# A graph and expert kernel: product of the router from raw rows, result biases kept in SBUF, last stage in groups of 3, 7 and 4 tiles

## The chip, the cores and the metric

The kernel runs on one core of a Trainium2 chip. The metric is the device time of one execution in microseconds (us), lower is better. Engines are written as in the profile: PE is TensorE, PEld its weight loads, DVE VectorE, ACT ScalarE, POOL GpSimd, SP SyncE, which here only starts transfers. A small q behind a name is that engine's instruction queue.

## The reference, cut to what matters

6250 nodes with 256 features and 200,000 edges. First comes a graph attention over the edges, then a mixture of 16 experts of which each node uses two.

```
x = x + gnn(layernorm(x), src, dst, edge_attr)       # edge stage, then one division per node and head
z = layernorm(x)
logits = z @ gate_w + gate_b                         # 6250 x 16
topk_vals, topk_idx = top_k(logits, 2);  topk_w = softmax(topk_vals)
h = relu(z @ w1[e] + b1[e])                          # 256 -> 512, for the two experts e of a node
expert_out = h @ w2[e] + b2[e]                       # 512 -> 256
y = z + sum over the two of topk_w * expert_out
x = x + layernorm(y) * gamma + beta
```

## The kernel before, in words

Nodes lie in 49 tiles of 128 rows; the last has 106 real rows. `token_rows` holds all of them in SBUF. All engines run queues of their own, in an order written by hand, and wait on counted semaphores. The stages follow each other:

*Edge stage.* Gathers rows for 200,000 edges and sums messages per node into `acc`. The diff doesn't touch it.

*Routing* (`stage_nodes`), seven groups i of seven tiles. ACT copies the sums to `staged` (L1027), four buffers; PE transposes them (L1076, `sums`); DVE divides (L1154) and adds the residual into `token_rows` (L1161), then takes statistics (L1228, L1234). ACT takes the square root (L1057), DVE the inverse, ACT writes the normalised rows `xn` (L1043), two buffers of seven tiles. PE transposes `xn` (L1108), ACT copies that (L1049), PE multiplies by the gate weights (L1093, `product`). DVE adds the gate bias (L1193) and finds the best two (`best_two`); PE counts how many rows go to each expert (`counts`), ACT copies the totals, DVE computes slots in HBM (`slots`), and POOL scatters the rows of the group to `dispatched` by 14 indirect transfers (L1011). In a step i, DVE does slots(i-1), attention and statistics(i+1), best_two(i), inverse(i+1); PE does counts(i-1), sums(i+1), router(i); ACT totals(i-1), stage(i+1), xn(i), the copies of i and deviation(i+1). `xn` of group i waits until the scatter of group i-2 has landed. SP loads b1, beta and the second weights of all experts (16 transfers of 512 KB, L962) once the last sums have been staged, because these lie in `shared`, in the place of `acc`. Then it stores 17 blocks of padding rows (L971).

*Experts* (`stage_experts`). 104 tiles of 128 dispatched rows, sorted by expert, in turns of four (R5). PE's step j: first layer of tile j+1 (L1512), transposition of the rows of j+2 (L1501), second layer of j (L1522). DVE's step j: rectified half of j+1, its flags and weights (L1548 to L1571), then for tile j the bias addition (L1577) and the weighting with the own row into `ys` (L1582). ACT does the other half, the own row (L1485) and copies. POOL scatters `ys` to `expert_rows` (L1375) and adds beta to `token_rows` (L1381) in 49 of the steps. SP's step j starts three transfers for tile j+3, in this order:

```
after(sp, s_h, j - R5 + 1);  first weights, 512 KB      # here j stands for the tile that is loaded
after(sp, s_t, ...); after(sp, s_bi, ...); after(sp, s_own, j - R5 + 1);  rows xs, 129.5 KB
after(sp, s_ys, j - R5 + 1);  result bias b2_t, broadcast to 128 partitions, 128 KB
```

Once in a turn SP reads eight numbers (experts and rows of four tiles) into registers (`load`, L1366); DVE, ACT and PE read one for every tile.

*Last stage.* In seven groups of seven tiles: SP loads the two expert rows of every node, `y0` and `y1`, two buffers deep. POOL adds four tiles (L1700); for the other three ACT copies `y1` to PSUM (L1679) and DVE adds (L1721). Statistics on DVE (L1728, L1734), square root (L1683), inverse, normalising on ACT (L1687) into four PSUM banks, gamma on DVE (L1744), the residual with beta on POOL (L1708), then SP stores.

## Time and profile before

| What | us |
|---|---|
| median of 3 runs | 2765.64 |
| lowest and highest | 2764.18, 2768.57 |
| the profiled execution | 2765.15 |
| span of its instructions | 2763.0 |
| PE busy | 943.2 |
| DVE busy | 1178.0 |
| ACT busy | 757.5 |
| POOL busy | 1794.8 |

The profiled execution is one more run; its span goes from the first to the last instruction. Busy times are summed over the whole span, most of which is the edge stage, so they say little on the stages that the diff touches. Those are read from stretches of the trace.

### The profile page before, as it was taken

Reading aid. Unit: us, or ns where it says so; the run is one execution under the profiler, and the core shown is the slowest. Engines: PE = TensorE matmul, PEld = TensorE weight load, DVE = VectorE, ACT = ScalarE, POOL = GpSimd, SP = SyncE. Lnnn points to the kernel's source line nnn. Section 1 sums busy time; section 2 is a strip of 40 time slices with the busy share of each in tenths; the row PEclk is TensorE's granted clock in tenths of the full one; section 3 lists DMA queues with packets and bytes.
Section 4 is the critical chain, followed back from the end, with each engine's and each line's share of the span. In section 5 each row is a group of like instructions: output and inputs, shape, how many; then the busy total and the mean of one; then the engine's idle time right before and its main releaser. Section 6 shows DMA issues by size and latency. Waiting matters only on the chain.

```text
span 2763.0 us, 40902 instructions
## 1 busy us (share of the span) xinstructions
PE 943.2 (34%) x6693; PEld 862.8 (31%) x6694; DVE 1178.0 (43%) x4381; ACT 757.5 (27%) x2809; POOL 1794.8 (65%) x1923
## 2 busy tenths in 40 slices
PE   6311222222222211122222222211126559899860
PEld 6211111111111111111111111111126458888850
DVE  5533333333333333333333333333347656666646
ACT  3222222222222222222222222222234323333334
POOL 3677777777777777777777777777735643333326
PEclk8555555555555555555555555555555579999985
DMA  5222222222222222222222222222212667676656
GB/s 170 60 57 56 56 57 56 56 57 56 56 57 56 56 57 56 56 56 56 56 57 56 57 56 56 57 56 56 57 28 78 216 204 222 213 220 217 218 183 225
DMA packets 191305, 260.90 MB, mean 94 GB/s; under 512 B 64374, under 2 KB 133047, under 8 KB 191140
## 3 DMA queue, kind: packets, MB, share of 16 engines
q0 software_dynamic: 59872, 135.05, 19.8%
q1 hardware_dynamic: 124980, 122.05, 14.4%
q10 hardware_dynamic: 6416, 3.41, 0.4%
q8 instruction: 11, 0.18, 0.0%
q14 instruction: 26, 0.21, 0.0%
HBM read 222.54 MB, written 38.69 MB: 95 GB/s over the span
## 4 chain that ended last, share of the span: by engine, by line
POOL 53%; issue 21%; PE 8%; DMA 6%; DVE 5%; SPq 4%; ACT 2%; POOLq 1%; DVEq 0%; ACTq 0%
POOL rows L206 52%; DMA xs<-dispatched 4%; SPq L1366 3%; PE p_y L1522 2%; PE p_h L1512 2%; PE p_l L1093 1%; POOL dispatched L1011 1%; ACT xn L1043 1%; PE p_tab L407 1%; DMA shared<-expert_rows 1%; DMA dispatched<-xn,slot_i 1%; ACT staged L1027 1%; PE p_t L1108 1%; PE p_x L1501 0%; SPq L1416 0%
## 5 line engine op out<-in xcount | busy, mean ns | idle before, releaser
L206 POOL DMA_INDIRECT rows<-node_table,index x1568 | 1480.2, 944 | 533.0 <-issue 477.3
L688 PE MATMUL p_win<-hot_ex,msg 128*65 128x64 f32 x3136 | 393.8, 319 | 1559.2 <-DVE hot_ex L801 1170.5
L688 PEld LDWEIGHTS p_win<-hot_ex,msg 128*65 128x65 f32 x3136 | 359.6, 229 | 1593.3 <-issue 1187.6
L723 ACT ACTIVATE p_part<-rows,attr_all 128x64 f32<-128x64 f32 x1568 | 388.4, 299 | 1495.2 <-DMA rows<-node_table,index 1495.2
L770 DVE TENSOR_TENSOR part<-rows,p_attr 128x544 f32<-128x544 f32 x196 | 141.3, 721 | 870.4 <-DMA rows<-node_table,index 868.8
L763 DVE TENSOR_TENSOR shared<-shared,p_win 65x64 f32 x784 | 171.0, 218 | 394.4 <-issue 312.7
L1375 POOL DMA_INDIRECT expert_rows<-ys,back x104 | 102.0, 981 | 308.6 <-DVE ys L1582 240.9
L1512 PEld LDWEIGHTS p_h<-xt,shared 128*128 128x128 f32 x1664 | 203.4, 193 | 5.4
L1512 PE MATMUL p_h<-xt,shared 128*128 128x128 f32 x1664 | 203.9, 276 | 0.0
L1522 PE MATMUL p_y<-shared,hid_t 128*128 x832 | 197.6, 381 | 0.0
L1522 PEld LDWEIGHTS p_y<-shared,hid_t 128*128 128x128 f32 x832 | 149.9, 190 | 16.3
L1011 POOL DMA_INDIRECT dispatched<-xn,slot_i x98 | 99.4, 1014 | 77.2 <-issue 41.5
L797 DVE TENSOR_TENSOR msg<-part,p_part 128x512 f32<-128x512 f32 x196 | 132.6, 677 | 0.0
L801 DVE TENSOR_TENSOR hot_ex<-hot,p_ex 128x512 f32<-128x512 f32 x196 | 132.6, 677 | 0.0
L1467 ACT ACTIVATE hid_t<-p_h,shared 128x128 f32<-128x128 f32 x208 | 64.9, 363 | 174.2 <-PE p_h L1512 174.1
L1548 DVE TENSOR_SCALAR hid_t<-p_h,shared 128x128 f32<-128x128 f32 x208 | 63.4, 346 | 96.4 <-PE p_h L1512 94.6
L1577 DVE TENSOR_TENSOR p_y<-p_y,b_t 128x256 f32<-128x256 f32 x104 | 45.0, 432 | 54.6 <-PE p_y L1522 54.0
L1501 PE MATMUL p_x<-ident,xs 128*128 128x128 f32 x208 | 42.0, 284 | 70.8 <-DMA xs<-dispatched 70.8
L1485 ACT ACTIVATE own<-xs,is_first 128x256 f32<-128x256 f32 x104 | 52.6, 506 | 27.2 <-DVE is_first L1559 25.9
L1582 DVE SCALAR_TENSOR_TENSOR ys<-p_y,weight,own 128x256 f32<-128x256 f32 x104 | 50.3, 484 | 20.8 <-DVE p_y L1577 20.6
L1454 ACT ACTIVATE xt<-p_x 128x256 f32<-128x256 f32 x104 | 39.9, 383 | 62.8 <-PE p_x L1501 62.8
L779 DVE TENSOR_TENSOR hot<-dst_rel,p_dve 128x128 f32<-128x128 f32 x196 | 54.8, 280 | 0.0
(221 smaller groups left out, 1254.0 us busy)
## 6 DMA issues: line engine op xcount, KB each, us to landing
shared<-in_w SPq DMA_DIRECT2D x120, 512.0 KB, 6.3
rows<-node_table,index POOLq DMA_INDIRECT x1568
xs<-dispatched SPq DMA_DIRECT2D x104, 129.5 KB
b_t<-in_b SPq DMA_DIRECT2D x104, 128.0 KB, 4.1
shared<-expert_rows SPq DMA_DIRECT2D x14, 768.0 KB, 6.3
out<-shared SPq DMA_DIRECT2D x6, 896.0 KB, 4.1
token_rows<-in_x SPq DMA_DIRECT2D x5, 896.0 KB, 7.2
index<-in_src SPq DMA_DIRECT2D x196, 4.0 KB, 1.6
```

What stands on the lines that cost most here:

```text
L206: pool.indirect_dma_start(out=rows[:, s, k, :], out_offset=None, in_=table, in_offset=bass.IndirectOffsetOnAxis(ap=index[:, s, k:k + 1], a ...
L688: last = pe.matmul(psum[0:MSG, u * HEADS * W:(u + 1) * HEADS * W], msg[:, v, k, :], weighted[:, k, :, :].rearrange("p h w -> p (h w)"), st ...
L723: last = act.activation(p_part[:, v, k, :], rows[:, s, k, COLS:COLS + HD], ACT.Copy, scale=attr_all[:, 1, ds(c * K + k, 1)])
L763: return dve.tensor_tensor(to, to, psum.rearrange("p (h w) -> p h w", h=HEADS), ALU.add)
L770: dve.tensor_tensor(part[:, :, :], rows[:, s, :, 0:COLS], attr_p[:, 0, :].unsqueeze(2).broadcast_to([P, K, COLS]), ALU.mult)\
L797: dve.tensor_tensor(msg[:, v, :, 0:HD], part[:, :, 0:HD], p_part[:, v, :, :], ALU.add)\
L801: dve.tensor_tensor(hot_ex[:, v, :, :, :], hot[:, :, :].unsqueeze(2).broadcast_to([P, K, HEADS, W]), ex_p.unsqueeze(3).broadcast_to([P, K, ...
L1011: pool.indirect_dma_start(out=dispatched, out_offset=bass.IndirectOffsetOnAxis(ap=slot_i[:, v, n:n + 1], axis=0), in_=xn[:, v, n // 2, :], ...
L1366: return nc.values_load_multi_w_load_instructions(of[:, ds(i * R5 + first, n)], engines=[eng.engine], min_val=0, max_val=most)[1]
L1375: pool.indirect_dma_start(out=expert_rows, out_offset=bass.IndirectOffsetOnAxis(ap=back[:, r, :], axis=0), in_=ys[:, r, :], in_offset=None ...
L1512: last = pe.matmul(p_h[:, u, f // 2, (f % 2) * P:(f % 2 + 1) * P], w1_r[:, r % R5, c, f * P:(f + 1) * P], xt[:, u, c, :], start=(c == 0), ...
L1522: last = pe.matmul(p_y[:, u, 0:D], hid_t[:, u, c, :], w2_sb[:, ds(e, 1), c, :] .rearrange("p a d -> p (a d)"), start=(c == 0), stop=(c == ...
```

## The change

Routing: the router's product is taken from `token_rows` before they are normalised. The gate weights are centred once (each column less its mean over the 256 features, by two matmuls of `ones` with the weights and one DVE instruction), and the logits are multiplied by the inverse deviation of the row ahead of the bias addition. PE's router waits for the residual (`s_x1`) instead of `xn`. Attention is cut in two parts of four and three tiles; the order on each queue is new, with staging up to two groups ahead; loops are unrolled.

Experts: the result biases of all 16 experts are loaded once, broadcast to 128 partitions (16 KB each), into `shared` ahead of the second weights. The load of `b2_t` for every tile and its wait on `s_ys` are gone from SP. DVE reads two expert numbers per tile instead of one, and adds the bias from SBUF by expert.

Last stage: groups of 3, six times 7, and 4 tiles; `y0` and `y1` three buffers deep; three of seven tiles are added on POOL, four on DVE; scalings by gamma alternate with the statistics of the next group; a square root at the start brings its table in; statistics have two buffers; gamma is waited for later.

```diff
+def unrolled(eng, step):
+
+    for i in range(NG):
+        step(i, i % 2, i // 2)
...
+        b2_at = tail + E * FC + D
+        b2_sb = shared[:, b2_at:b2_at + E * D].rearrange("p (e d) -> p e d", e=E)
...
+            sp.dma_start(g["b2_sb"], g["b2"].rearrange("(a e) d -> a e d", a=1).rearrange("a e d -> (a e) d")
+                         .partition_broadcast(P)).then_inc(g["s_b2"], 16)
             for e in range(E):
                 sp.dma_start(g["w2_sb"][:, e, :, :], g["w2"][e].rearrange("(c p) d -> p c d", p=P))\
...
-                if not first(i):
-                    dispatch(i - 1, 1 - v)
-
...
-            alternate(pool, step)
-            dispatch(NG - 1, 0)
+            unrolled(pool, step)
...
+            def transposed(i):
...
+            def normalised(i, v, k):
+                act.wait_ge(s_rc, 2 * i + 2)
+                after(act, sent[v], 16 * G * k)
+                for u in range(U):
+                    act.activation(xn[:, v, u, 0:D], tile_row(token_rows, i * U + u), ACT.Identity,
+                                   bias=nmr[:, u:u + 1], scale=rstd[:, u:u + 1]).then_inc(s_nm, 1)
+
+            def step(i, v, k):
                 if not final(i):
+                    stage(i + 1, GB, U)
+                totals(i)
+                if not final(i):
+                    transposed(i + 1)
+                    if not final(i + 1):
+                        stage(i + 2, 0, GB)
                     deviation(i + 1)
+                    normalised(i + 1, 1 - v, k + v)
 
             def deviation(i):
                 act.wait_ge(s_mv, i + 1)
                 act.activation(rstd[:, :], mv[:, :, 1], ACT.Sqrt, bias=eps[:, 0:1]).then_inc(s_sd, 1)
-            stage(0)
+            stage(0, 0, U)
+            transposed(0)
+            stage(1, 0, GB)
             deviation(0)
-            alternate(act, step)
-            totals(NG - 1)
+            normalised(0, 0, 0)
+            unrolled(act, step)
...
+            pe.wait_ge(s_in, 32)
+            for c in range(KC):
+                last = pe.matmul(p_n[:, 0, 0:E], ones[:, :], gate_w_sb[:, c, :], start=(c == 0), stop=(c == KC - 1))
+            last.then_inc(s_gs, 1)
...
+            def router(i):
+                after(pe, s_lg, 2 * i - 1)
                 for u in range(U):
                     t = i * U + u
-                    pe.wait_ge(s_nm, t + 1)
+                    pe.wait_ge(s_x1, t + 1)
                     after(pe, s_xc, t - reuse(u, 2, U) + 1)
                     for c in range(KC):
                         last = pe.transpose(p_t[:, u % 2, c * P:(c + 1) * P],
-                                            xn[:, v, u, c * P:(c + 1) * P], ident[:, :])
+                                            tile_row(token_rows, t, c * P, P), ident[:, :])
                     last.then_inc(s_xt, 1)
                     if u:
                         product(i, u - 1)
                 product(i, U - 1)
-            sums(0)
-            pe.wait_ge(s_in, 32)
+
+            def step(i, v, k):
+                counts(i)
+                if not final(i):
+                    sums(i + 1, GB, U)
+                    router(i + 1)
+                    if not final(i + 1):
+                        sums(i + 2, 0, GB)
+            sums(0, 0, U)
+            pe.wait_ge(s_gate, 1)
+            router(0)
+            sums(1, 0, GB)
             pe.wait_ge(s_c, CONSTANTS)
-            alternate(pe, step)
-            counts(NG - 1)
+            unrolled(pe, step)
 
         @block.vector
         def _(dve):
...
+            dve.wait_ge(s_gs, 1)
+            dve.scalar_tensor_tensor(out=gate_w_sb[:, :, :], in0=p_n[:, 0, 0:E].unsqueeze(1).broadcast_to([P, KC, E]),
+                                     scalar=-1.0 / D, in1=gate_w_sb[:, :, :], op0=ALU.mult, op1=ALU.add)\
+               .then_inc(s_gate, 1)
...
+            def attention(i, q):
+                for a, b in GROUPS[q:q + 1]:
...
             def best_two(i, v, k):
                 dve.wait_ge(s_l, (i + 1) * U)
                 dve.tensor_tensor(logits[:, :, :], p_l[:, 0:U * E].rearrange("p (u e) -> p u e", e=E),
+                                  rstd[:, :].unsqueeze(2).broadcast_to([P, U, E]), ALU.mult)\
+                   .then_inc(s_lg, 1)
+                dve.wait_ge(s_lg, 2 * i + 1)
+                dve.tensor_tensor(logits[:, :, :], logits[:, :, :],
                                   gate_b_sb[:, :].unsqueeze(1).broadcast_to([P, U, E]), ALU.add)\
                    .then_inc(s_lg, 1)
-                dve.wait_ge(s_lg, i + 1)
+                dve.wait_ge(s_lg, 2 * i + 2)
...
             def step(i, v, k):
-                if not first(i):
-                    slots(i - 1, 1 - v)
-                if not final(i):
-                    attention(i + 1, 1 - v, k + v)
-                    statistics(i + 1, 1 - v)
                 best_two(i, v, k)
                 if not final(i):
+                    attention(i + 1, 0)
+                slots(i, v)
+                if not final(i):
+                    attention(i + 1, 1)
+                    statistics(i + 1, 1 - v)
                     inverse(i + 1)
-            attention(0, 0, 0)
+            attention(0, 0)
+            attention(0, 1)
             statistics(0, 0)
             inverse(0)
             dve.wait_ge(s_in, 32)
             dve.wait_ge(s_c, CONSTANTS)
-            alternate(dve, step)
...
-            def fetch_rows(j, r, e, row):
+            def fetch_rows(j, r, row):
                 after(sp, s_t, j - R5 + 1)
                 after(sp, s_bi, j - R5 + 1)
                 after(sp, s_own, j - R5 + 1)
                 sp.dma_start(xs[:, r, :], dispatched[ds(row, P), :]).then_inc(s_xs[r], 16)
-                after(sp, s_ys, j - R5 + 1)
-                sp.dma_start(b2_t[:, r, :], g["b2"][ds(e, 1), :].rearrange("a d -> (a d)")
-                             .partition_broadcast(P)).then_inc(s_b2[r], 16)
 
             def step(j, r, i, last):
...
-            def finish(j, r, i):
+            def finish(j, r, e):
                 dve.wait_ge(s_y, j + 1)
-                dve.wait_ge(s_b2[r], 16 * (i + 1))
-                dve.tensor_tensor(p_y[:, r % 2, 0:D], p_y[:, r % 2, 0:D], b2_t[:, r, :], ALU.add)\
+                dve.tensor_tensor(p_y[:, r % 2, 0:D], p_y[:, r % 2, 0:D], tile_row(b2_sb, e), ALU.add)\
...
             def step(j, r, i, last):
-                if not behind(r, last, 1):
-                    front(j + 1, (r + 1) % R5, i + (r + 1) // R5, load(dve, expert_of_tile, i, r + 1, 1)[0])
-                finish(j, r, i)
+                if behind(r, last, 1):
+                    e, = load(dve, expert_of_tile, i, r, 1)
+                else:
+                    e, coming = load(dve, expert_of_tile, i, r, 2)
+                    front(j + 1, (r + 1) % R5, i + (r + 1) // R5, coming)
+                finish(j, r, e)
+            dve.wait_ge(s_b2, 16)
             dve.wait_ge(s_b1, 16)
...
-        ON_POOL = 4
-        RN = 4
...
+        LOADED, STORED, KEPT, SUMS = 3, 2, 4, 4
+        spots = [0, 3] + [3 + U * m for m in range(1, NG)] + [NT]
+        count = len(spots) - 1
+        tiles = [range(a, b) for a, b in zip(spots, spots[1:])]
+        on_pool = [len(ts) * 3 // U for ts in tiles]
...
+        y0, y1, out_rows = room(0, LOADED), room(LOADED, LOADED), room(2 * LOADED, STORED)
...
+            def load(n):
+                v = n % LOADED
+                if n >= LOADED:
+                    sp.wait_ge(s_nm, spots[n - LOADED + 1])
+                for a, b, real in pieces(n):
+                    for to, of, done in ((y0, expert_rows[0:NP], s_y0), (y1, expert_rows[NP:2 * NP], s_y1)):
+                        sp.dma_start(to[0:real, v, a - spots[n]:b - spots[n], :], dram(of, a, b, real))\
+                          .then_inc(done[v], 16)
+
+            def store(n):
+                sp.wait_ge(s_f, spots[n + 1])
+                for a, b, real in pieces(n):
+                    sp.dma_start(dram(g["out"], a, b, real),
+                                 out_rows[0:real, n % STORED, a - spots[n]:b - spots[n], :])\
+                      .then_inc(s_out[n % STORED], 16)
+
...
+            load(0)
+            sp.dma_start(gamma[:, :], g["gamma"].partition_broadcast(P)).then_inc(s_g, 16)
+            for n in range(1, LOADED):
+                load(n)
+            for n in range(count):
+                if n + LOADED < count:
+                    load(n + LOADED)
+                store(n)
+            for n in range(count - STORED, count):
+                sp.wait_ge(s_out[n % STORED], stored(n))
...
+            act.wait_ge(returned, 1)
+            act.activation(table_for[:, :], eps[:, :], ACT.Sqrt)
+            second_rows(0)
+            deviation(0)
+            for n in range(count):
+                if n + 1 < count:
+                    second_rows(n + 1)
+                act.wait_ge(s_rc, 2 * n + 2)
+                for t in tiles[n]:
+                    u = t - spots[n]
+                    after(act, s_gm, t - KEPT + 1)
+                    act.activation(p_norm[:, t % KEPT, 0:D], y0[:, n % LOADED, u, :], ACT.Identity,
+                                   bias=nmr[:, n % 2, u:u + 1], scale=rstd[:, n % 2, u:u + 1]).then_inc(s_nm, 1)
+                if n + 1 < count:
+                    deviation(n + 1)
...
+            add_rows(0)
+            for n in range(count):
+                if n + 1 < count:
+                    add_rows(n + 1)
+                for t in tiles[n]:
+                    row = out_rows[:, n % STORED, t - spots[n], :]
                     pool.wait_ge(s_gm, t + 1)
-                    pool.tensor_tensor(out_rows[:, v, u, :], out_rows[:, v, u, :], tile_row(token_rows, t), ALU.add)\
...
+            sums(0)
+            for u in range(len(tiles[0])):
+                statistics(0, u)
+            moments(0)
+            inverse(0)
...
-            alternate(dve, step)
+            for n in range(count):
+                if n >= STORED:
+                    dve.wait_ge(s_out[n % STORED], stored(n - STORED))
+                if n + 1 < count:
+                    sums(n + 1)
+                    held = len(tiles[n]) - 2
+                    for u in range(max(held, len(tiles[n + 1]))):
+                        if u < held:
+                            scaled(n, spots[n] + u)
+                        if u < len(tiles[n + 1]):
+                            statistics(n + 1, u)
+                    moments(n + 1)
+                    for t in tiles[n][held:]:
+                        scaled(n, t)
+                    inverse(n + 1)
+                else:
+                    for t in tiles[n]:
+                        scaled(n, t)
 
```

## Rows read from the trace of the kernel before

**Rows 1.** Stretches: length, busy us of PE, PEld, DVE, ACT, POOL, clock, DMA share, GB/s.
```profile
2101.00:2121.00 20.00, 13.32 (x74) 11.94 (x74) 14.63 (x72) 10.17 (x23) 14.42 (x15) 0.50 0.27 96
2337.00:2437.00 100.00, 89.96 (x609) 83.14 (x608) 62.85 (x260) 38.24 (x119) 32.56 (x36) 1.00 0.68 215
2637.00:2671.00 34.00, 32.55 (x220) 30.39 (x219) 20.02 (x98) 13.63 (x42) 8.45 (x9) 1.00 0.56 187
2699.09:2735.93 36.84, 0.00 (x0) 0.00 (x0) 29.67 (x104) 18.92 (x44) 29.61 (x44) 0.50 0.88 299
```
**Rows 2.** Waits of PE, 2237 to 2672: us in total, times, longest.
```profile
PE p_x L1501 <- DMA xs<-dispatched: 38.7, 30, 1.8
```

**Rows 3.** Timeline of PE, experts, first two and last second layers: start, length, instruction.
```profile
2242.93 1.89 PE L1522 MATMUL p_y<-shared,hid_t 128*128 x8
...
2246.67 1.89 PE L1522 MATMUL p_y<-shared,hid_t 128*128 x8
...
2667.87 3.62 PE L1522 MATMUL p_y<-shared,hid_t 128*128 x16
```

**Rows 4.** Chain that ended last, experts, one turn of SP: start, length, what.
```profile
2387.51 0.33 SPq L1425
...
2388.25 0.87 SPq L1366
...
2392.94 3.94 DMA xs<-dispatched
```

**Rows 5.** DVE's register reads, line 1366: ns least/median/most, first and last start.
```profile
L1366 DVEq TENSOR_LOAD <-expert_of_tile x103: 300/306/373, 2243.2 to 2667.0; - x103
```

**Rows 6.** Timeline of DVE and POOL, experts.
```profile
2384.49 0.63 DVE L1556 TENSOR_TENSOR second<-xs,expert_f 128x1 f32<-128x1 f32 x1
...
2385.01 0.75 POOL L1381 TENSOR_TENSOR token_rows<-token_rows,shared 128x256 f32 x1
...
2388.65 0.15 DVE L1556 TENSOR_TENSOR second<-xs,expert_f 128x1 f32<-128x1 f32 x1
```

**Rows 7.** Timeline of routing, first and last groups; in brackets idle time before.
```profile
2054.19 1.28 ACT L1057 ACT_TABLE_LOAD   x1
2054.45 1.56 PE L1076 MATMUL p_g<-ident,staged 65*128 65x65 f32 x12 [1.08 <-DVE attn L1154]
...
2063.44 3.73 ACT L1027 ACTIVATE staged<-shared 65x512 f32<-65x512 f32 x7
...
2068.89 1.06 PE L1108 MATMUL p_t<-ident,xn 128*128 128x128 f32 x4
...
2078.72 0.27 DVE L1193 TENSOR_TENSOR logits<-p_l,gate_b_sb 128x112 f32<-128x112 f32 x1 [2.41 <-PE p_l L1093]
...
2086.18 1.03 POOL L1011 DMA_INDIRECT dispatched<-xn,slot_i  x1 [35.69 <-DVE slot_i L1189]
...
2187.21 3.55 ACT L1043 ACTIVATE xn<-token_rows,nmr,rstd 128x256 f32<-128x256 f32 x7 [6.93 <-DMA dispatched<-xn,slot_i]
...
2206.87 1.14 POOL L1011 DMA_INDIRECT dispatched<-xn,slot_i  x1 [5.34 <-issue]
```

**Rows 8.** Timeline of SP, end of routing.
```profile
2165.11 27.21 SPq L962 DMA_DIRECT2D shared<-in_w  x16
2207.86 13.58 SPq L971 DMA_DIRECT2D dispatched<-pad_row  x16
...
2232.70 0.35 SPq L1423 DMA_DIRECT2D xs<-dispatched  x1
```

**Rows 9.** Timeline of SP, start of the last stage.
```profile
2675.85 2.41 SPq L1653 DMA_DIRECT2D shared<-expert_rows  x4
```

**Rows 10.** Chain that ended last, last stage.
```profile
2678.30 6.84 DMA gamma<-in_gamma
...
2731.99 9.78 DMA shared<-expert_rows
...
2753.53 0.68 POOL shared L1708
```

More of the change, by code:

```diff
@@ L1257, in _ @@
             dve.wait_ge(s_c, CONSTANTS)
[L1258 to L1259 removed]
+            unrolled(dve, step)
             dve.tensor_copy(run_end[:, :], total[0:1, :, 0]).then_inc(s_run, 1)
@@ L1621, in stage_experts @@
         s_f = sem("final_ready")
[L1622 to L1642 removed]
+        s_out = [sem(f"final_stored{v}") for v in range(STORED)]
```

216 lines of the change are left out of this document (82 added, 134 removed).

## Prediction

> **What bounds the kernel now.** The edge stage comes first and the diff doesn't touch it. Behind it lie routing, experts and the last stage. I read first one table of stretches, a row for each of these parts [rows 1], which shows how full each engine is, then for each part the view that says what its waits waited for.
>
> *Routing.* In a stretch of 20.00 us, one group of seven tiles, no engine is full: VectorE 14.63 us, GpSimd 14.42, ScalarE 10.17, TensorE 13.32 [rows 1]. A chain over all of them sets the pace: stage, normalise, router product, best two, slots. The seven dispatches begin at 2086.18 first and 2206.87 last, 20.1 apart on average; the last waited 5.34 us, because ScalarE's normalising at 2187.21 had waited 6.93 us for older dispatches to land [rows 7].
>
> *Experts.* TensorE is 90% busy over 100 us and 96% over the last 34 us, at clock 1.00 [rows 1]. Its second layers start 3.74 us apart when nothing is late, but from 2242.93 to 2667.87 there are 102 steps (the last row holds two tiles), 424.94 us or 4.17 each [rows 3]. The one thing TensorE waits for is a tile's rows from HBM: 38.7 us in 30 waits [rows 2]. The chain tells why they come late. SP issues the bias load of a tile only after VectorE's result four tiles back, here at 2387.51; in every fourth step it then reads eight registers, from 2388.25 on, and the next rows leave at 2392.94 and land 3.94 us later [rows 4].
>
> *Last stage.* A group of seven takes 36.84/4 = 9.21 us; VectorE is busy 29.67/4 = 7.42 of it, GpSimd 7.40, DMA 0.88 at 299 GB/s [rows 1]. It begins at 2675.85 with the first load [rows 9]; from there to the end of the span (2763.0) are 87.15 us.
>
> **The change, part by part.** The profiled execution took 2765.15 us, 2.15 more than its span; the median of the runs is 2765.64, so 0.5 more than the sum below.
>
> *Experts: bias loads gone.* 104 loads of 128 KB leave SP, and with them its wait for the result. SP then stops only for the scatter index and the own row of the same tile four back. These come ahead of that tile's second layer, bias addition and weighting, so about one tile step (3.7 us) before the result. The register reads, from 2388.25 to about 2392.1 (2392.94 less 0.8 for issuing the weights), stay, but start that much earlier. The longest wait of TensorE is 1.8 us [rows 2], so one step of advance covers each. To be had: 424.94 - 102 x 3.735 = 44.0 us (38.7 recorded, the rest is restarting). What is late next? The second layer needs VectorE. It is busy 62.85 us in 24 tiles, 2.6 us each [rows 1], and its queue reads one register between them, 0.31 us [rows 5] or 0.5 with what follows. The change reads two; SP's eight take 3.9 us, so 0.48 more [rows 4]. Sum 2.6 + 0.5 + 0.48 = 3.58, under 3.735. Small instructions are stretched beside GpSimd's beta addition of 0.75 us, 0.63 where 0.15 is usual [rows 6], but the 2.6 us hold these. VectorE may fall behind by some 3 us before TensorE, which works one tile ahead, feels it. I charge 2 us and take 42. Bounds: 30 (waits between add 0.3, VectorE at 3.87: 104 x 0.135 = 14 lost) and 44.
>
> The Trainium skill, page "SBUF — State Buffer", section "SBUF: two separate sides", says that a VectorE instruction with two SBUF inputs and a GpSimd instruction that reads SBUF exclude each other for the whole instruction. The trace agrees [rows 6]. If by that rule the 49 beta additions met VectorE in full and today meet it in none, 49 x 0.75 us would come on top, 0.35 a tile: pitch 3.93 and, with 3.735 as the floor, 24 instead of 44 us gained.
>
> *Routing: product from raw rows.* The router now starts when a tile's residual is there, not after statistics, a staging of seven tiles and a normalising. Two matmul pairs on the gate weights and one VectorE instruction on 32 elements are added at the very start, beside the head maximum: 1 us on an idle TensorE, hidden; without that cover 1 us once. First group: TensorE ends its transposes at 2054.45 + 1.56 = 2056.0, and the router took from 2068.89 to 2078.72, 9.8 us [rows 7]; now it ends at about 2065.9. ScalarE then stages four tiles (2.1 us, from 3.73 for seven) and must load the square root's table (1.28), which it had done in idle time [rows 7]; deviation and inverse take 0.8 by estimate. So best-two starts at about 2068.5 instead of 2078.72. It is one multiply longer (0.4), and four tiles of attention (3.4) now stand ahead of the slots, where only counts and totals stood: of the 10.2 us gained some 7 are left, and the first dispatch starts at 2079. The pace: VectorE 14.63 + 0.3 busy, plus the tail in which it waits while ScalarE copies the last tiles, stages four and takes deviations, 3.5 us, and small waits: about 18.7. The floor is GpSimd's own 14.42 us busy in 15 instructions with 0.3 between, 14 x 1.28 = 17.9, the ceiling today's 19.5 for undisturbed groups. The last dispatch would start at 2079 + 6 x 18.7 = 2191, 16 us earlier. The landing wait goes: xn is normalised about 5 us after its buffer's older dispatch has landed.
>
> But the experts wait for SP's queue too. SP issues the second weights from 2165.11, throttled, for 27.21 us; then 13.58 us of padding stores; four us of registers; first weights; then the first rows at 2232.70 [rows 8]. The new 16 x 128 KB bias copy (2.1 MB) goes ahead of the weights. At their rate, 8.4 MB in 27.21 us = 308 GB/s, it is 6.8 us; at 385 GB/s, 5.5; if it hides in the queue, 0. Staging of the last tile moves 3 us later. Today SP has slack until 2207.86; then 2168.4 + 27.2 + 5.5 = 2201.1, + 13.6 + 4.5 + 1.7 = 2220.9 for the first rows. GpSimd's side would be ready at 2191 + 20 + 6 = 2217. SP ends last: 2232.7 - 2220.9 = 11.8. I take 11.5; bounds 5 (pace stays at 19.5, copy at 6.8 and queued weights in the way) and 18 (copy hidden, pace 17.9).
>
> *Last stage.* Seven equal groups, two buffers become eight groups (3, six of 7, 4), three buffers. First data: 2.0 MB with gamma landed by 2685.16, 9.3 us after the issue, and VectorE's first wait was for gamma [rows 10]. Now group 0 and group 1 (2.75 MB) land at +11.6, by 3.5 us fixed and 0.34 MB/us. Four additions 1.5, statistics and one scaling 2.7, moments 0.8, two scalings 0.7, inverse 0.5: the group after the first is normalised at +18; today's stretch from 2699.09 on [rows 1] begins with the second group's normalising, +23.2. Pace: VectorE 7.42 + one addition 0.36 + waits 0.4 = 8.2, since the scalings no longer stand alone behind ScalarE. DMA would need 2.75 MB in 8.2 us = 336 GB/s, and 299/0.88 = 340 is what today's mix allows [rows 1]: close. So +18 + 5 x 8.2 = +59, + 6 for the four-tile group = +65, + 3.9 to the last GpSimd addition = +68.9. Today that addition ends at 2754.21, and 8.8 us follow [rows 10]. Fewer tiles in the last store take 1 us off: 7.8. End at +76.7 against +87.15: 10.5 gained. Bounds 4 (pace 9.2 kept, since the transfers bind; head start alone) and 15 (pace 7.4).
>
> The last tile has 106 rows. Its load landed 9.78 us after the issue, though the whole first group and gamma needed 9.3 [rows 10]. The Trainium skill, page "DMA: Bandwidth & Descriptors", section "Why a DMA increments its semaphore by 16 and not by 1", says that a transfer is spread over the largest number of engines up to 16 that divides the slowest dimension, so over two for 106. The trace agrees with the slow landing. The load is now hidden, but by that rule the final store keeps its slow piece, and the tail would shrink by under 1 us, not by the share of bytes.
>
> Sum: 42 + 11.5 + 10.5 = 64; 2765.15 - 64 + 0.5 = **2701.6**.
>
> **Rivals.**
> 1. *VectorE becomes the experts' bound.* For it: the second register and the stretched instructions. Against: it is idle ahead of most rectified layers today. At 3.87 to 3.95 us a tile the stage gains 30 to 22: total 2714 to 2722.
> 2. *The copy of all biases costs nothing, or the last stage reaches 7.5 us.* For it: SP's issue is limited by what is in flight, and large rows may move better. Routing 17, last stage 14: 42 + 17 + 14 = 73, so 2692.
> 3. *Last stage and routing keep their pace*, because transfers bind (DMA already 0.88) and ScalarE stands between: 42 + 5 + 4 = 51, so 2715.
> 4. *Slower than before.* TensorE has no pause left and its clock is lowered to 1.2 GHz for part of the expert stage. Each tile at half clock costs 3.7 us more; it decides from 17 of 104 tiles on (64/3.7); for the whole stage 385 - 64 = 320 more, 3085. Against it: 34 us at 96% busy kept clock 1.00 [rows 1].
> 5. *The change does not do what it says:* rows stay late because the own-row flag stops SP as the result did. Then 11.5 + 10.5 alone: 2744.
>
> **Chances.** Forecast 0.50, rival 1 0.15, rival 2 0.12, rival 3 0.13, rival 5 0.06, rival 4 0.03, a rest of 0.01. Some 0.2% (5.5 us) is what a measurement of this kernel can tell from no change. Faster 0.95, same 0.02, slower 0.03. Range 2687 to 2723: it leaves out rivals 4 and 5 and the edges of 1 and 2.
>
> **What the profile after would show.** TensorE's waits for xs near zero and second layers 3.74 us apart throughout; if VectorE binds, even pitches near 3.9 and TensorE waiting for hid_t. First dispatch at about 2079, pitches near 18.7, first rows issued by SP at 2221, and SP rather than GpSimd ahead of it in the chain. Last stage: 8.2 us a group and no wait for shared<-expert_rows after the second group. The prediction fails if pitches in the experts exceed 3.85 us, if the new copy holds the weights for over 8 us, or if loads in the last stage come late three deep.

## The result, and the profile after

The changed kernel takes 2717.57 us (median of 4 runs, 2716.79 to 2718.72) against 2765.66 for the kernel before on the same chip: ratio 0.9822, 95% interval 0.9806 to 0.9837. That is 48.1 us gained, where the sum of the prediction was 64. The span fell from 2763.0 to 2715.0 us. By stage, with the first rows' load and the first load of the last stage as borders:

```
                                   before     after   change  forecast
start to the first rows' load     2232.70   2217.74   -15.0    -11.5
experts, to the last stage's load   443.15    421.76  -21.4    -42
last stage, to the end of the span   87.15     75.50  -11.65   -10.5
```

So two terms were right within 4 us, and the largest came to half of what was forecast. The kernel before had a span of 2763.0 us, so the three changes add up to 48.0.

**Experts.** The waits of TensorE, 2217 to 2640 us (total, times, longest), then those of SP in the same stage:

```profile
PE p_x L1531 <- DMA xs<-dispatched: 49.3, 1, 49.3
PE p_h L1542 <- ACT xt L1484: 6.4, 20, 0.7
```
```profile
SPq L86 <- ACT own L1515: 164.4, 76, 3.5
```

The 30 waits for rows [rows 2] are gone but for the stage's start; SP now stops for the own row (`s_own`) and comes early enough. Yet the second layers did not go back to 3.73 us. Timeline of TensorE, the first two and the last three of them (the last three are tiles 102 to 104):

```profile
2230.21 1.89 PE L1552 MATMUL p_y<-shared,hid_t 128*128 x8
...
2233.94 1.89 PE L1552 MATMUL p_y<-shared,hid_t 128*128 x8
...
2626.94 1.89 PE L1552 MATMUL p_y<-shared,hid_t 128*128 x8
...
2630.45 1.89 PE L1552 MATMUL p_y<-shared,hid_t 128*128 x8
...
2633.05 1.99 PE L1552 MATMUL p_y<-shared,hid_t 128*128 x8 [0.70 <-issue]
```

From 2230.21 to 2630.45 are the same 102 steps as in [rows 3]: 400.24 us, 3.92 each instead of 4.17. The first seven pitches are 3.73, then a turn of four repeats, mostly 3.73, 4.01, 3.87 and 4.26, until GpSimd makes its last addition of beta at 2580.64; from 2585.61 on all but one (4.02) are 3.73 again. VectorE's timeline shows one such turn; its rectified layers (L1578) start 4.11, 3.96, 3.57 and 4.23 us apart:

```profile
2401.70 0.61 DVE L1578 TENSOR_SCALAR hid_t<-p_h,shared 128x128 f32<-128x128 f32 x2 [1.03 <-PE p_y L1552]
...
2405.81 0.61 DVE L1578 TENSOR_SCALAR hid_t<-p_h,shared 128x128 f32<-128x128 f32 x2 [1.56 <-PE p_y L1552]
2406.34 0.52 DVE L1586 TENSOR_TENSOR second<-xs,expert_f 128x1 f32<-128x1 f32 x1
...
2409.77 0.61 DVE L1578 TENSOR_SCALAR hid_t<-p_h,shared 128x128 f32<-128x128 f32 x2 [1.04 <-issue]
...
2413.34 0.61 DVE L1578 TENSOR_SCALAR hid_t<-p_h,shared 128x128 f32<-128x128 f32 x2 [1.03 <-PE p_y L1552]
2413.87 0.39 DVE L1586 TENSOR_TENSOR second<-xs,expert_f 128x1 f32<-128x1 f32 x1
...
2414.36 0.57 DVE L1591 SCALAR_TENSOR_TENSOR back<-second,xs 128x1 int32<-128x1 f32 x1
```

The step of 3.57 us is VectorE by itself, with 1.03 idle ahead of the rectified layer, in which its queue reads two tile numbers into registers. What stands on the line of that read (`load`, L1399) in VectorE's queue, besides the read itself (525 ns, see experiment 4), for 104 tiles:

```profile
L1399 DVEq FUSED_REGOPS  x208: 75/190/190, 2230.5 to 2634.7; - x104
L1399 DVEq SEQ_ASSERT  x207: 23/23/33, 2230.7 to 2635.0; - x104
```

Each value that is read brings one operation on registers of 190 ns and one assertion of 23 ns with it, two of each a tile. Once a turn the idle time is 1.56, because the loop's end is in it (+0.53). And beside additions of beta, `second` takes 0.52 or 0.39 and `back` 0.57 instead of 0.15. Four times 3.57 + 0.53 is 14.81, just under TensorE's 14.93; with the stretched instructions (0.37 + 0.24 + 0.42 = 1.03) it is 15.84, and TensorE's four pitches are 15.87. The profile puts these waits down to TensorE or to "issue"; that they have the same length with either name is a sign that they are the queue's own, and the chain that ended last agrees: from 2398 to 2418 us nothing but VectorE and its queue is on it.

VectorE holds TensorE up by way of ScalarE, whose copy of the transposed rows (`xt`) stands in its queue behind `own` and `odds`, and both wait for VectorE. From the same table of waits as above:

```profile
ACT own L1515 <- DVE is_first L1589: 197.3, 102, 2.7
PEld p_h L1542 <- ACT xt L1484: 28.1, 62, 1.1
```

**Routing.** SP's timeline, the first dispatch of GpSimd and the first of its last group, and the chain of waits:

```profile
2159.42 0.49 SPq L972 DMA_DIRECT2D shared<-in_b  x1
2159.95 35.04 SPq L975 DMA_DIRECT2D shared<-in_w  x16
2197.07 13.45 SPq L984 DMA_DIRECT2D dispatched<-pad_row  x16
...
2217.74 1.39 SPq L1456 DMA_DIRECT2D xs<-dispatched  x3
```
```profile
2076.70 1.03 POOL L1020 DMA_INDIRECT dispatched<-xn,slot_i  x1 [27.45 <-DVE slot_i L1219]
...
2184.93 1.76 POOL L1020 DMA_INDIRECT dispatched<-xn,slot_i  x1 [0.30 <-issue]
```
```profile
2210.56 7.03 DMA dispatched<-pad_row
2217.74 4.97 DMA xs<-dispatched
```

Set beside [rows 7, 8]: the first dispatch came 9.5 us earlier, the groups follow each other at GpSimd's own pace (0.30 us between dispatches, 18.0 a group), and SP's padding stores are what lands last. One of ScalarE's normalisings still waited for older dispatches, for nearly as long as before (6.93 us in [rows 7]), but GpSimd was not held up by it:

```profile
2174.70 3.55 ACT L1056 ACTIVATE xn<-token_rows,nmr,rstd 128x256 f32<-128x256 f32 x7 [5.80 <-DMA dispatched<-xn,slot_i]
```

The second weights now take 35.04 us of SP instead of 27.21.

**Last stage.** SP's timeline with the first load, and the chain of waits:

```profile
2639.50 0.91 SPq L1691 DMA_DIRECT2D shared<-expert_rows  x2
```
```profile
2641.46 10.43 DMA shared<-expert_rows
...
2672.93 7.18 DMA out<-shared
...
2687.93 8.62 DMA out<-shared
2696.57 1.08 DVE shared L1771 x3
```

The second group's rows landed at +12.4 us, and the chain waits twice for a store. ScalarE starts a group's normalising at 2658.55, 2665.56, 2672.58, 2679.93 and 2687.57: pitches of 7.01 to 7.64 us.

### The profile page after: what moved, and what is told of

It reads as the page before. It is cut to its first block, busy times and chain, and to the rows that moved or that the text cites. A ratio compares the mean times of both kernels' runs of the same rounds, so it can differ in the third digit from the quotient of the medians.

```text
span 2715.0 us, 40328 instructions
## 1 busy us (share of the span) xinstructions
PE 948.6 (35%) x6697; PEld 855.9 (32%) x6698; DVE 1161.4 (43%) x4399; ACT 761.7 (28%) x2819; POOL 1789.0 (66%) x1915
## 4 chain that ended last, share of the span: by engine, by line
POOL 53%; issue 22%; DVE 10%; PE 5%; DVEq 4%; DMA 2%; SPq 2%; ACT 1%; POOLq 1%; ACTq 0%
POOL rows L215 52%; DVEq L1399 3%; PE p_h L1542 2%; PE p_y L1552 2%; SPq L975 1%; DVE p_y L1606 1%; DVE hid_t L1578 1%; DVE second L1586 1%; DVE back L1591 1%; DMA out<-shared 1%; DVE first_w L1599 0%; DVE attn L1184 0%; DMA node_table<-rows 0%; DVE stats L491 0%; PE p_tab L416 0%
## 5 line engine op out<-in xcount | busy, mean ns | idle before, releaser
L1542 PE MATMUL p_h<-xt,shared 128*128 128x128 f32 x1664 | 211.1, 281 | 6.8 <-ACT xt L1484 6.4
L1578 DVE TENSOR_SCALAR hid_t<-p_h,shared 128x128 f32<-128x128 f32 x208 | 63.4, 347 | 152.8 <-PE p_y L1552 77.1
L1497 ACT ACTIVATE hid_t<-p_h,shared 128x128 f32<-128x128 f32 x208 | 65.1, 364 | 12.0 <-PE p_h L1542 10.2
L737 ACT ACTIVATE p_ex<-score,neg_shift 128x32 f32<-128x32 f32 x196 | 52.9, 270 | 0.0
```

What stands on the lines that cost most here:

```text
L1542: last = pe.matmul(p_h[:, u, f // 2, (f % 2) * P:(f % 2 + 1) * P], w1_r[:, r % R5, c, f * P:(f + 1) * P], xt[:, u, c, :], start=(c == 0), ...
L1578: last = dve.tensor_scalar(hid_t[:, u, c, :], p_h[:, u, 1, (c - FC // 2) * P:(c - FC // 2 + 1) * P], b1_sb[:, ds(e * FC + c, 1)], 0.0, ALU ...
```

## The experiments

Times are medians. The ratio to the kernel before is over runs on the same chip, and "against the changed kernel" compares with its 2717.57 us on another chip of about the same speed, except for the last four rows.

```
                  us       before    ratio (95%)
experts alone     2739.38  2767.75   0.9901 (0.9885-0.9918)
last stage alone  2756.09  2767.75   0.9954 (0.9937-0.9970)
one read          2696.98  2767.75   0.9744 (0.9728-0.9761)
no beta           2697.36  2767.75   0.9744 (0.9728-0.9761)
three reads       2750.71  2769.66   0.9930 (0.9914-0.9947)
pads on ScalarE   2718.27  2769.66   0.9812 (0.9795-0.9828)
three stores      2715.36  2769.66   0.9805 (0.9789-0.9821)
combined          2693.49  2769.66   0.9721 (0.9705-0.9737)
late copy         3333.31  3401.59   0.9794 (0.9778-0.9810)
routing alone     3374.93  3401.59   0.9921 (0.9904-0.9937)
late, combined    3307.43  3401.59   0.9724 (0.9708-0.9741)
the same again    3312.41  3406.16   0.9727 (0.9714-0.9740)
```

The kernel before took 2765.66, 2767.75 and 2769.66 us on the first three chips, so a difference "against the changed kernel" is uncertain by 1 to 3 us; by the ratios, the padding stores on ScalarE would come out 2 us under the changed kernel and three stores 5 under. Lengths of stages within one profile are given where a small difference matters. They scatter too: the experts' stage of the kernel before took 443.15 us in its own profile and 447.88, with the same code, in that of the last stage alone.

**1. The parts alone.** The experts' part in the kernel before (with the copy of all result biases in SP's queue), and the last stage in the kernel before.

> The kernel before with the experts' part of the change alone (the result biases in SBUF, SP no longer waiting for the result, VectorE reading two registers a tile, and the 2 MB copy of the biases in SP's queue of the routing stage). My theory: the experts' stage gains the 21 us that it gained in the whole change (pitch of the second layers 3.73 us in the first seven tiles, then about 3.97), and the routing stage loses 4 to 8 us, because the copy stands in SP's queue ahead of the second weights and the padding rows: in all 13 to 18 us under the kernel before. Rival: the copy costs the routing stage nothing, since there GpSimd's queue is later than SP's: then 20 to 22 us under the kernel before.

> The kernel before with the last stage of the change alone. Theory: the parts are independent, so this gains the 11.7 us that the last stage lost in the whole change (10.5 to 12.5). Rival: part of those 11.7 us was due to a better start, because the experts' rows had landed earlier in a run with faster experts: then under 9 us.

Measured: 28.4 us and 11.7 us gained. The last stage is as the theory said: the interval, 8 to 17 us, is wide, but in the profile it takes 75.05 us, as in the changed kernel (75.50), against 87.15. The experts' part gained more than either number, yet the rival's mechanism holds: the first rows left at 2232.52 instead of 2232.70, though the edge stage had ended 0.9 us earlier, so the copy cost under 1 us there. SP's timeline of the kernel with the experts' part alone:

```profile
2164.60 35.72 SPq L973 DMA_DIRECT2D shared<-in_w  x16
2207.25 13.77 SPq L982 DMA_DIRECT2D dispatched<-pad_row  x16
```

The weights take 8.5 us longer (27.21 in [rows 8]), but SP waits until 2207.25 for the ends of the runs anyway. In the changed kernel that slack is gone and the same copy lies on the path. So the parts are not independent: 28.4 + 11.7 of 48.1 leaves 8 us for the new routing order, though it moved the first rows by 15. By spans the experts' part gave 26.0 us (2763.0 to 2737.0), 25.6 of it in its own stage, which is 4.2 more than that stage gained in the changed kernel. Most of this difference is lost at the start of the experts, 12.5 us from the first rows' load to the first second layer in the changed kernel against 9.1 here and 10.2 in the kernel before. The remaining 2.4 us of the 28.4 are about the difference between the chips' times of the kernel before (2767.75 and 2765.66).

**2. One register read a tile.** The tile number that VectorE read for the next tile is kept for that tile's own bias addition.

```
 def step(j, r, i, last):
-    if behind(r, last, 1):
-        e, = load(dve, expert_of_tile, i, r, 1)
-    else:
-        e, coming = load(dve, expert_of_tile, i, r, 2)
-        front(j + 1, ..., coming)
+    if r == 0:
+        read["e"] = load(dve, expert_of_tile, i, 0, 1)[0]
+    e = read["e"]
+    if not behind(r, last, 1):
+        read["e"] = load(dve, expert_of_tile, i, r + 1, 1)[0]
+        front(j + 1, ..., read["e"])
     finish(j, r, e)
```

> The changed kernel, but VectorE reads one tile number a tile and keeps the other in its register (two only at the first of each turn of four). Theory A, VectorE's serial order bounds the experts' stage: each register read that is gone from the chain takes 0.2 to 0.5 us from about 75 of the 104 tiles: 12 to 25 us under the changed kernel, with the pitch of the second layers back near 3.75. Theory B, the beta additions of GpSimd, which stretch VectorE's operations, are what holds the pitch: then under 5 us. Theory C, TensorE's waits for ScalarE's copy hold it: no change.

Measured: 20.6 us under the changed kernel. All pitches but one (4.22) and the last are 3.73 or 3.74 us, and TensorE waits for next to nothing behind the start. Its waits, then the stretch that answers to the second of [rows 1]:

```profile
PE p_x L1531 <- DMA xs<-dispatched: 49.7, 1, 49.7
PE p_h L1542 <- ACT xt L1484: 0.2, 1, 0.2
```
```profile
2337.00:2437.00 100.00, 100.00 (x700) 94.51 (x700) 68.73 (x298) 43.20 (x135) 36.23 (x41) 1.00 0.64 209
```

Theory A holds; B and C, as they were put, do not. The clock stayed at 1.00, that is 2.4 GHz, with TensorE busy all the time.

**3. No beta.** The lines with `with_beta` and the wait for them are removed. This kernel leaves the addition of beta out.

> The changed kernel without GpSimd's additions of beta beside the experts (that part of the computation is left out: beta is never added). Theory A (VectorE's reads and their queue): VectorE's operations are shorter by 0.1 to 0.25 us a tile, and the stage by 5 to 12 us, the pitch staying above 3.8. Theory B (contention between GpSimd's additions and VectorE is the whole loss): the pitch falls to 3.73 in all tiles and the stage by 20 us or more.

Measured: 20.2 us under the changed kernel, pitches of 3.73 to 3.74 throughout. That is theory B's number, and theory A's size for this run was wrong. The two removals give the same gain, so neither cause is "the whole loss": the reads and the stretching stand in one serial chain, and taking out either brings it under TensorE's pace. The groups of VectorE's instructions from 2260 to 2600 us say how (busy total and mean ns, idle time before them): the changed kernel,

```profile
L1578 DVE TENSOR_SCALAR hid_t<-p_h,shared 128x128 f32<-128x128 f32 x172 | 52.4, 347 | 100.9 <-PE p_y L1552 70.4 <-issue 30.5
L1611 DVE SCALAR_TENSOR_TENSOR ys<-p_y,weight,own 128x256 f32<-128x256 f32 x86 | 41.6, 484 | 17.5 <-DVE p_y L1606 17.5
...
L1586 DVE TENSOR_TENSOR second<-xs,expert_f 128x1 f32<-128x1 f32 x86 | 25.1, 292 | 0.0
L1591 DVE SCALAR_TENSOR_TENSOR back<-second,xs 128x1 int32<-128x1 f32 x86 | 21.1, 245 | 0.0
```

and without beta,

```profile
L1586 DVE SCALAR_TENSOR_TENSOR back<-second,xs 128x1 int32<-128x1 f32 x91 | 13.6, 150 | 0.0
...
L1581 DVE TENSOR_TENSOR second<-xs,expert_f 128x1 f32<-128x1 f32 x91 | 13.6, 149 | 0.0
```

The stretching is (292 - 149) + (245 - 150) = 0.24 us a tile. Per tile VectorE then needs 3.57 + 0.53/4 + 0.24 = 3.94 us in the changed kernel (measured pitch 3.92), and 3.70 without beta, under TensorE's 3.73. With one read the idle time ahead of the rectified layer is 0.55 instead of 1.03 in three tiles of four, and 1.66 to 1.89 where the turn begins, with two reads and the loop's end; that is some 0.85 instead of 1.17 on average, so VectorE needs about 3.6.

**4. Three reads.** VectorE reads three tile numbers at a time and drops the third (`load(dve, expert_of_tile, i, r, 2 if last else 3)[0:2]`).

> The changed kernel, but VectorE reads three tile numbers at a time and drops the third. Theory: VectorE's own serial order is the pace (four tiles: 4 x 3.57 us alone, 0.53 for the end of the turn, 1.05 beside two beta additions, 15.87 together), and one read more costs what e3_one_read gave back a tile, 0.48 us of idle time before the rectified layer (1.03 against 0.55). All 104 tiles then pay, the ones without additions too: pitches of 17.8 us for four, total 45 to 50 us over the changed kernel, 2763 to 2768. Rival: the read overlaps VectorE's last instruction, and only what sticks out counts: under 25 us.

Measured: 33.1 us over the changed kernel, between the theory's number and the rival's. The same groups of VectorE:

```profile
L1578 DVE TENSOR_SCALAR hid_t<-p_h,shared 128x128 f32<-128x128 f32 x158 | 48.1, 346 | 127.7 <-issue 127.7
...
L1586 DVE TENSOR_TENSOR second<-xs,expert_f 128x1 f32<-128x1 f32 x79 | 21.2, 269 | 0.0
...
L1591 DVE SCALAR_TENSOR_TENSOR back<-second,xs 128x1 int32<-128x1 f32 x79 | 11.8, 149 | 0.0
```

Idle time before the rectified layer is 127.7/79 = 1.62 us a tile instead of 100.9/86 = 1.17, so one more value costs 0.44 (1.53 instead of 1.03 in most tiles, 1.86 instead of 1.56 at the loop's end), close to the 0.48 of the theory. But the shift moved VectorE's small instructions against GpSimd's additions, and `back` no longer meets them: 0.12 us less. 3.94 + 0.44 - 0.12 = 4.26; the second layers are 4.25 us apart. The theory's 45 to 50 us left out that stretching changes with the phase, and that TensorE's floor hid part of it in the first seven tiles and the last fifteen. The register read itself (VectorE's reads of the tile numbers: least, median, most ns) in the kernel with one, the changed one with two, and this with three:

```profile
L1399 DVEq TENSOR_LOAD <-expert_of_tile x130: 299/311/575, 2196.6 to 2610.8; - x130
```
```profile
L1399 DVEq TENSOR_LOAD <-expert_of_tile x105: 316/525/639, 2195.2 to 2634.4; - x105
```
```profile
L1399 DVEq TENSOR_LOAD <-expert_of_tile x105: 311/746/1101, 2194.2 to 2668.2; - x105
```

The step is 0.21 to 0.22 us a register. The Trainium skill, page "Runtime: NRT & Kernel Launch", section "Instruction fetch mechanics", gives about 200 ns a register for loads of registers from HBM. Here the numbers come from SBUF, and the trace shows the same step. The engine loses 0.44 to 0.48 us for each value, twice as much, and the queue's rows under the heading Experts say why: 0.21 for the read, 0.19 for the operation on registers and 0.02 for the assertion that follow it make 0.42, and the pauses between them are the rest.

**5. Padding stores on ScalarE's queue.**

```
-sp.wait_ge(s_run, 1)
-sp.wait_ge(s_c, CONSTANTS)
-for e in range(0, E, 4):
-    ... sp.dma_start(dispatched[ds(row, P), :], pad_row[:, :]) ...
 unrolled(act, step)
+act.wait_ge(s_run, 1)
+act.wait_ge(s_c, CONSTANTS)
+for e in range(0, E, 4):
+    ... act.dma_start(dispatched[ds(row, P), :], pad_row[:, :]) ...
```

> The changed kernel with the 17 padding stores issued by ScalarE's queue, which is empty from 2178.49 us on (the ends of the runs are known at 2181.4), instead of by SP behind the second weights. Theory: SP's queue ends the routing stage. SP is then done with the weights at 2195, and what is left is GpSimd: last dispatch at 2204 plus 6 to 7 us of landing, so the first rows leave at about 2211 instead of 2217.7: 6 to 8 us under the changed kernel. Rival 1: the padding stores share the DMA engines with the weights and only move the wait: 0 to 3 us. Rival 2: GpSimd ends the stage at the same time as SP anyway: 0.

Measured: 0.7 us over the changed kernel, no difference; rival 1 holds and my theory falls. Timelines of SP and ScalarE, and the chain:

```profile
2161.30 47.59 SPq L975 DMA_DIRECT2D shared<-in_w  x16
```
```profile
2184.79 16.32 ACTq L1077 DMA_DIRECT2D dispatched<-pad_row  x16
```
```profile
2201.13 17.25 DMA dispatched<-pad_row
2218.54 7.10 DMA xs<-dispatched
```

The padding stores were issued by 2201, ten us earlier, but the last took 17.25 us to land instead of 7.03, and the issue of the weights stretched from 35.04 to 47.59 us. From the head maximum to the first rows are 169.17 us, against 169.71 in the changed kernel. GpSimd's last dispatch began at 2205.5, and the slowest of its dispatches took 10.1 us to land, so rival 2 would have let the rows go by about 2216 at the latest (an estimate), 2.5 us before they did. Stretches of the kernel before, then of the changed kernel, say what the transfers were doing (the DMA share is the number before the last):

```profile
2195.00:2205.00 10.00, 4.38 (x21) 3.85 (x21) 4.94 (x34) 1.50 (x4) 5.00 (x6) 0.50 0.57 210
2205.00:2212.00 7.00, 0.00 (x0) 0.00 (x0) 6.76 (x10) 0.00 (x0) 4.22 (x4) 0.50 0.37 118
```
```profile
2195.00:2205.00 10.00, 0.00 (x0) 0.00 (x0) 0.07 (x1) 0.00 (x0) 7.78 (x8) 0.50 1.08 350
2205.00:2212.00 7.00, 0.00 (x0) 0.00 (x0) 0.00 (x0) 0.00 (x0) 0.00 (x0) 0.50 1.10 196
```

The DMA engines had slack there before and are full now. So at the end of routing neither queue sets the time but the work already handed to the DMA engines: 8.4 MB of second weights, 2.1 MB of biases, the padding rows and the dispatches.

**6. Three store buffers** (`STORED` from 2 to 3) in the last stage.

> The changed kernel with three instead of two buffers for the stores of the last stage. VectorE waited 2.9 us for stores there. Theory: the store buffers hold VectorE back: 2 to 3 us under the changed kernel. Rival: the transfers themselves are the pace (DMA share 1.08 and 1.02 in the stretches from 2670 and 2680), and the stores that come sooner only delay loads: within 1 us of the changed kernel.

Measured: 2.2 us under the changed kernel in the medians, within what the runs can tell (the intervals overlap). The profile is clearer: the last stage takes 72.97 us instead of 75.50, VectorE no longer waits for a store, and over 37 us from 2661 it is busy 35.79 instead of 33.66:

```profile
2661.00:2698.00 37.00, 0.00 (x0) 0.00 (x0) 35.79 (x139) 25.56 (x62) 35.10 (x52) 0.50 0.94 322
```

VectorE, 97% busy, is then the fullest engine, with the DMA share at 0.94; which of the two binds, no run here separates.

**7. Combined:** one read, padding stores on ScalarE, three store buffers.

> e3_one_read, e6_pads_on_act and e7_stored3 in one kernel. Theory: they lie in three stages and add up, 20.6 from the reads, 6 to 8 from the padding stores and 0 to 3 from the store buffers: 2686 to 2691. Rival: TensorE, now 3.73 us a tile without a pause, or its clock, takes part of it back: over 2692.

Measured: 2693.49 us, 2.5 to 7.5 above the theory, in which the padding stores were to give 6 to 8. The number lies in the rival's range, but not for the rival's reason: from 2240 to 2600 us TensorE was busy 359.98 us at clock 1.00, and the experts' stage took 402.15 us against 401.06 with one read. It is the fastest kernel of those measured on chips of this speed: 24.1 us under the changed kernel, 76.2 under the kernel before.

**8. The copy of the biases later.** Its line in the routing stage moves behind the experts' first three `fetch_rows`, and VectorE's wait for it behind the first `front`. Two more kernels go with it: the routing part in the kernel before, without any such copy, and a combination with the late copy, one read and three store buffers, which was measured twice.

> The changed kernel with the 2 MB copy of the result biases issued behind the first three tiles' rows instead of ahead of the second weights; VectorE waits for it ahead of the first bias addition. Theory, after e6_pads_on_act: what ends the routing stage is the bytes that the DMA engines still have before them, not the queue that issues them. With 2 MB fewer ahead, the second weights are issued in 27 instead of 35 us, the padding stores end at about 2203, and then GpSimd's last dispatch (2204 plus 6 to 7 us of landing) sets the first rows at 2211: 5 to 8 us under the changed kernel, less up to 2 us when the copy meets the first tiles' weights and rows. Rival: GpSimd's dispatches end as late, or the copy holds up the first tiles by as much as it gave: 0 to 2 us.

> The kernel before with the routing part of the change alone, and so without the copy of the result biases. Theory: the first rows leave at about 2211 as in e9_b2_late, 21 us earlier than before, and the rest keeps its length: 19 to 23 us under the kernel before. Rival: the 15 us that the routing stage gained in the whole change are all that the new order gives, whatever the bytes: 13 to 16 us.

> e3_one_read, e7_stored3 and e9_b2_late in one kernel, to beat both. Theory: 20.6 and 2.2 us as measured apart, and 5 to 8 from the late copy: 2687 to 2690. Rival: at the faster pace of the experts the late copy costs the first tiles what it saves in the routing stage: 2693 to 2696, as e8_combined.

> The kernel of e11_best once more, because on the chip that ran e9 to e11 the kernel before took 3401 us instead of 2766, in stages that the diff does not touch too, so that its routing stage can't be set beside the others'. Theory (bytes ahead of the rows end the routing stage): from the head maximum to the first rows 161 to 164 us instead of the 169.2 to 169.7 of e3_one_read and e8_combined, no more than 2 us given back at the first tiles, in all a ratio to before of 0.970 to 0.972. Rival (the copy only moves the wait): 168 us and more, or as much lost up to the first second layer, ratio 0.973 to 0.974.

For all four the kernel before took 3401 or 3406 us on the same chip as they did, and one of these two chips had given 2769.66 earlier. So only ratios count here, and the stages can't be set beside the others: the head maximum, behind an edge stage that no kernel here changes, came at 2632.1 us instead of 2048, and from the first to the last dispatch GpSimd took 164.5 us (2660.8 to 2825.3) instead of 127.3. In the kernel with the late copy the second weights were all issued by 2800.6 and SP then waited until 2810.83 for the ends of the runs, so there the bytes can't be what ends the routing. From the head maximum to the first rows are 200.48 us there, and 199.76, 198.38 and 201.51 in the other three: neither number of the last expectation (161 to 164, or 168) can be tested on that. Nor can the routing part alone be judged by its two expectations: it gained 26.7 us, more than either, in stages longer than they were meant for. What these runs do show: without the copy in front the weights were issued in 24.79 us; and the combination with the late copy has 0.9724 and 0.9727, the earlier one 0.9721, so no gain shows; 0.9727 lies between the two ratios that the last expectation set apart. Whether the late copy gives the 5 to 8 us at the usual speed stays open.

## Why the prediction was right or wrong

**Experts (forecast 42, measured 21.4): rival 1 happened.** The prediction's own sign of failing, pitches over 3.85 us, came: they are 3.92. The other two did not: the copy held the weights for 7.8 us, and in the last stage only the first loads are waited for. The mechanism of the gain was right: the bias loads were what made rows late, the own-row flag comes early enough (rival 5 falls), and TensorE kept its clock (rival 4 falls). The step that failed is "Sum 2.6 + 0.5 + 0.48 = 3.58, under 3.735". Busy time was charged enough: 62.30 us over 100/3.92 = 25.5 tiles is 2.44 each, stretching included, where 2.6 was charged. What was missing is idle time that VectorE's own order makes: 17.5/86 = 0.20 us between bias addition and result, some 0.10 in the small chain, and 1.17 ahead of the rectified layer where 0.98 was charged, the loop's end among it. That is 3.91, as measured. The first two stood in the trace before (16.7 us over 81 tiles and 2.8 us three times over), hidden since VectorE waited for TensorE then; the third is longer by the second value and could only be worked out. The bound "waits between add 0.3, VectorE at 3.87" named them and I gave them too little weight. TensorE did not wait for `hid_t`, as the sign of rival 1 had it, but for ScalarE's copy.

The total of rival 1, 2714 to 2722, holds the measured 2717.6, and that is partly luck: its stage was to gain 22 to 30 us and gained 21.4, and the other two stages gave 4.7 us more than forecast. The same 4.7 brought the forecast of 2701.6 nearer to the result than its largest term was.

**The rule on shared access.** The prediction priced full mutual exclusion at 0.35 us a tile, on top of a kernel before in which none of it was met. That premise was wrong: in the kernel before, from 2260 to 2600 us, `second` took 0.374 and `back` 0.348 on average, which is 0.42 us a tile above the 0.149 and 0.150 without beta. Shown in the changed kernel: 0.24 us a tile, with 41 additions in 86 tiles about 0.5 us for each addition of 0.75. Only instructions with two SBUF inputs are stretched (`second`, `back`; in the kernel with one read `change` too, 0.23), and `is_first`, with one, keeps 0.154. So on which instructions meet, the rule of the page "SBUF — State Buffer", section "SBUF: two separate sides", of the Trainium skill and the trace agree.

**Routing (forecast 11.5, measured 15.0).** First dispatch 2079 against 2076.70, pace 18.7 against 18.0: GpSimd's own floor. 1.2 us of it is an edge stage that ended earlier (head maximum 2048.03 against 2049.26). The landing wait, which the prediction said would go, stayed at 5.80 us in one group, and cost nothing, because GpSimd had dispatches of the group before to issue. The copy was charged 5.5 us and stretched the weights by 7.8. That SP's stores come last in the chain was right, but "SP ends last" as a reason was not: the kernel with the padding stores on ScalarE and a DMA share of 1.08 and 1.10 show that what they waited for is the transfers. 2.2 us were given back at the start of the experts (12.47 against 10.23 us to the first second layer), where the first rows took 4.97 us to land.

**Last stage (forecast 10.5, measured 11.65).** The landing was forecast at +11.6 and came at +12.4, and the second group's normalising at +19.1 where +18 was forecast. The pace was better, 7.0 to 7.6 instead of 8.2, as rival 2 had it: the scalings slip between the statistics without a wait. Some of that was lost to stores, two deep, which the prediction did not look at, and the tail stayed at 8.8 us instead of 7.8.

## What to carry to other kernels

Taking a wait away from an engine at 90% brings the next engine's serial order to light, so add up that order from start to start (idle gaps between dependent instructions, register reads, the loop's end) and not from busy time. Two delays in one chain with little slack each look like the whole cause when removed alone; run both removals before naming one. When two queues share the DMA engines, moving an issue to an idle queue moves nothing if the bytes are the bound; look at the DMA share first. And a read of a register is not one instruction: count what stands on its line in the queue.

## What was not expected of the hardware

A value that this program reads into a register of VectorE's queue costs the engine 0.44 to 0.48 us, of which the read is 0.21 and an operation on registers and an assertion behind it another 0.21. TensorE stood at 2.4 GHz through 100 us of 100% busy time. And one chip ran the kernel before in 2769.66 and later in 3406.16 us. The profile of the kernel with the late copy, at that lower speed, has VectorE's queue at 26% of the chain of waits instead of 4% (24% in two more at that speed; the chain of the fourth covers only part of its span), and its expert stage as long as ever (422.8 us against 421.8); the runs do not show why.
